# A six-stage transformer block on one core: the head of the first stage, the stores and the routing rearranged

## The reference, cut to what matters

```python
x = x + 0.5 * gated_moe(layernorm(x))     # 2 experts, top 1, silu(x Wg) * (x Wu), then Wd, FF 1024
x = x + attention(layernorm(x))           # 16 heads of 16, causal, softmax
x = x + 0.5 * gated_moe(layernorm(x))     # the same weights
x = x + 0.5 * moe(layernorm(x))           # 8 experts, top 2, logits = gelu(x rw1) @ rw2, gelu FF 1024
x = x + mixer(layernorm(x))               # a state-space mixer
x = x + 0.5 * moe(layernorm(x))           # the same weights as in stage 4
```

## Time and profile before

| | us |
|---|---|
| runs, median of 3 | 994.5 (992.1 to 997.3) |
| the profiled execution | 990.16 |
| its span | 988.3 |
| stage 1, gated MoE with weight preparation | to about 151 |
| stage 2, attention | to about 333 |
| stage 3, gated MoE | to about 452 |
| stage 4, MoE of 8 experts | to about 631 |
| stage 5, mixer | to about 804 |
| stage 6, MoE of 8 experts | to the end |

### The profile page before, as it was taken

One profiled execution on the slowest core, in us unless ns is written; L12 is line 12 of the kernel. 1 busy time (PEld: TensorE's weight loads), 2 busy tenths in 40 slices (PEclk: granted clock), 3 DMA queues, 4 the chain that ended last, 5 costly groups with the idle time before them and its releaser, 6 DMA issues.

```text
span 988.3 us, 21269 instructions
## 1 busy us (share of the span) xinstructions
PE 845.4 (86%) x7784; PEld 551.6 (56%) x7785; DVE 615.4 (62%) x1132; ACT 428.9 (43%) x990; POOL 337.2 (34%) x400
## 2 busy tenths in 40 slices
PE   3089988978888789998989999897889879999995
PEld 2046553423333336664689999544344444999993
DVE  5635646678993436654646565676798746555655
ACT  6434435136767515444244444367211152544440
POOL 2212114050000211112344553224888632555530
PEclk9999989989999879997799999999999997999997
DMA  8326622531104214422487664300000003666644
GB/s 292 130 86 213 220 73 75 174 109 48 27 20 172 78 32 144 131 94 92 163 335 242 239 226 155 100 1 1 0 1 0 1 30 115 252 242 238 226 156 142
DMA packets 46296, 125.38 MB, mean 127 GB/s; under 512 B 10202, under 2 KB 23467, under 8 KB 40207
## 3 DMA queue, kind: packets, MB, share of 16 engines
q0 software_dynamic: 13392, 67.96, 19.6%
q1 hardware_dynamic: 26698, 49.36, 15.2%
q10 hardware_dynamic: 6132, 7.05, 2.2%
HBM read 97.28 MB, written 26.71 MB: 125 GB/s over the span
## 4 chain that ended last, share of the span: by engine, by line
PE 57%; DVE 13%; DMA 9%; ACT 8%; POOL 6%; issue 6%; SPq 1%; ACTq 0%; DVEq 0%; POOLq 0%
PE psum L567 16%; PE psum L540 12%; PE psum L526 7%; PE psum L1347 3%; DMA stage<-in_w 3%; DVE mem L1472 2%; PE psum L114 2%; POOL mem L2137 2%; POOL mem L2133 2%; PE psum L513 1%; DMA mem<-xn_dram,mem 1%; PE psum L1900 1%; PE psum L1844 1%; DVE mem L312 1%; DMA max_dram<-mem 1%
## 5 line engine op out<-in xcount | busy, mean ns | idle before, releaser
L567 PE MATMUL psum<-mem 128*128 x1536 | 180.9, 275 | 3.2 <-DVE mem L808 1.9
L567 PEld LDWEIGHTS psum<-mem 128*128 128x128 f16 x1536 | 147.4, 98 | 24.4 <-issue 4.3
L540 PE MATMUL psum<-mem 128*128 128x128 f16 x2208 | 132.0, 220 | 0.0
L916 POOL DMA_INDIRECT y_dram<-mem x64 | 63.5, 993 | 194.5 <-DVE mem L824 194.5
L658 ACT ACTIVATE mem<-psum,mem 128x128 f32<-128x128 f32 x368 | 105.0, 369 | 54.3 <-PE psum L540 52.8
L540 PEld LDWEIGHTS psum<-mem 128*128 128x128 f16 x2208 | 128.1, 98 | 0.7
L911 POOL DMA_INDIRECT mem<-xn_dram,mem x64 | 66.7, 1042 | 120.5 <-PE psum L513 92.4
L1432 ACT ACTIVATE mem<-psum 128x512 f32<-128x512 f32 (+1 forms) x160 | 79.9, 552 | 54.3 <-PE psum L1327 35.5
L526 PE MATMUL psum<-mem 128*128 x432 | 100.3, 390 | 2.2 <-issue 2.2
L114 PE MATMUL psum<-ones 128*128 128x512 f16 x312 | 97.9, 440 | 0.6 <-issue 0.6
L1472 DVE TENSOR_REDUCE mem<-psum 128x2 f32<-128x1024 f32 (+2 forms) x96 | 87.6, 950 | 15.8 <-PE psum L1293 8.7
(11 more groups left out here) (246 smaller groups left out, 1382.1 us busy)
## 6 DMA issues: line engine op xcount, KB each, us to landing
stage<-in_w SPq DMA_DIRECT2D x32, 512.0 KB, 4.0
w_rows<-mem SPq DMA_DIRECT2D x8, 1024.0 KB, 7.6
xn_dram<-mem ACTq DMA_DIRECT2D x32, 128.0 KB, 1.7
mem<-y_dram SPq DMA_DIRECT2D x16, 256.0 KB, 5.2
mem<-in_w_gate SPq DMA_DIRECT2D x4, 512.0 KB, 6.7
mem<-in_w_up SPq DMA_DIRECT2D x4, 512.0 KB, 10.6
mem<-in_w_down SPq DMA_DIRECT2D x4, 512.0 KB, 14.0
mem<-y_dram SPq DMA_DIRECT2D x16, 128.0 KB, 3.4
```

Of the source, the lines that this page charges most:

```text
L540: ins = eng.matmul(c.bank(2 * p + j // half)[:, j % half * P:(j % half + 1) * P], mats[q][:, l, k, j * P:(j + 1) * P], x[:, p, k, :], star ...
L567: ins = eng.matmul(c.bank(6)[:, 0:D], a[:, 0 if gated else p, q * half + j, :], w[:, at], start=(i == 0), stop=(i == 3 * CF - 1))
L916: eng.indirect_dma_start(c.y_dram[:, :], bass.IndirectOffsetOnAxis(ap=yidx[:, b:b + 1], axis=0), yo[:, b % 2, :], None).then_inc(s_ys[b % ...
```

## The change

First stage. VectorE prepares gate and up, then does `block_x(0)` and `block_x(1)`, and only then the down matrix; TensorE's `block_ready` asks for gate and up alone, and the second product waits for down. The four attention matrices join `split1`, which now has 21 chunks; of each step's chunks the first two are handled where they were, a third behind `block_x` on ScalarE and behind `block_y` on VectorE. No store of w1 rows stands among the loads: the first is issued ahead of the attention stage, three behind its last maxima.

Routing. The router's matmuls go partly between the layer norm's transposes; ranks are computed with fewer and wider matmuls; the last expert's column is left out of the comparison and the clamp with it; the one-hot is made by two `tensor_tensor` on f16; activation tables are asked for early by an activation on one unused column.

Attention. The first key projection goes between the layer norm's transposes; GpSimd stores the first group of projected rows, SyncE only the second; stack 2 is asked for after the second half of pair 0's maxima has landed; `keep_awake` goes from 12 to 2 and from 2 to 1 a piece.

```diff
@@ layernorm_stage
     def act(eng):
+        if table is not None:
+            eng.activation(c.spent[:, 0:1], c.ln_consts[:, 0:1], table)
...
             ins.then_inc(s_tps.sem, 1)
+            worked = between(eng, i) if between is not None else 0
             if "idle_bank" in src:
-                keep_awake(c, eng, src["idle_bank"], 3)
+                keep_awake(c, eng, src["idle_bank"], 3 - min(worked, 2))
@@ moe_stage
+    def router_between(eng, i):
+        if i == 4:
+            for ready in W["router_ready"]:
+                eng.wait_ge(*ready)
+        if gated:
+            if i >= 4:
+                for n in ((0, 1, 2) if i == 4 else (i - 2,)):
+                    router_tile(eng, n)
+            return 0
+        if i < 5:
+            return 0
+        eng.wait_ge(*L["lo"](NT // 2))
+        ins = router_half(eng, 0, range(2 * (i - 5), 2 * (i - 4)))
+        if i == NT - 1:
+            ins.then_inc(s_hid.sem, 1)
+        return 2
...
-            for s in range(HALVES):
-                eng.wait_ge(*L["lo"]((s + 1) * NT // HALVES))
...
+            eng.wait_ge(*L["lo"](NT))
+            router_half(eng, 1, range(len(ROUTER))).then_inc(s_hid.sem, 1)
...
-        for t in range(NT):
-            out = c.bank(5)[:, NE + t * E:NE + (t + 1) * E]
-            todo = [(c.before16, k, t) for k in range(TOPK)] + [(c.ones16, k, u) for u in range(t) for k in range(TOPK)]
-            for i, (m, k, u) in enumerate(todo):
-                ins = eng.matmul(out, m[:, :], mk[:, k, u, :], start=(i == 0), stop=(i == len(todo) - 1))
+        ranks = c.bank(5)[:, NE:2 * NE].rearrange("p (t e) -> p t e", e=E)
+        for k in range(TOPK):
+            ins = eng.matmul(ranks, c.before16[:, :], mk[:, k, :, :], start=(k == 0), stop=False, skip_group_check=True)
+        for u in range(NT - 1):
+            for k in range(TOPK):
+                ins = eng.matmul(ranks[:, u + 1:NT, :], c.ones16[:, :], mk[:, k, u, :].unsqueeze(1).to_broadcast([P, NT - 1 - u, E]),
+                                 start=False, stop=(u == NT - 2 and k == TOPK - 1), skip_group_check=True)
...
+        if weights_act is None:
+            eng.activation(c.spent[:, 1:2], c.ln_consts[:, 0:1], ACT.Silu if gated else ACT.Gelu)
...
-        eng.tensor_scalar(ebi[:, :], ebf[:, :], float(E - 1), None, ALU.min).then_inc(s_eb.sem, 1)
         if not gated:
-            link(eng.tensor_scalar(spare[:, :], ebf[:, :], float(E - 1), float(P), ALU.min, ALU.mult))
-            eng.tensor_scalar(widx[:, :], spare[:, :], c.row_spare[:, :], float(1 + TOP2 * T), ALU.add, ALU.subtract).then_inc(s_wi.sem, 1)
-            eng.wait_ge(*s_wi(1))
+            eng.tensor_scalar(widx[:, :], ebf[:, :], float(P), c.row[:, :], ALU.mult, ALU.add).then_inc(s_wi.sem, 1)
+        eng.tensor_copy(ebi[:, :], ebf[:, :]).then_inc(s_eb.sem, 1)
...
-        for i in range(KT):
-            eng.tensor_scalar(oh[:, i, :], c.iota_p[:, :], pcol[:, i // NT, i % NT:i % NT + 1], None, ALU.is_equal)\
-                .then_inc(s_oh.sem, 1)
+        columns = pcol[:, :, :].rearrange("p k t -> p (k t)")
+        for i in range(2):
+            part = slice(i * KT // 2, (i + 1) * KT // 2)
+            eng.tensor_tensor(oh[:, part, :], c.iota16[:, 0:P].unsqueeze(1).to_broadcast([P, KT // 2, P]),
+                              columns[:, part].unsqueeze(2).to_broadcast([P, KT // 2, P]), ALU.is_equal).then_inc(s_oh.sem, 1)
...
         block_x(0, 0)
         block_x(1, 1)
+        if weights_late is not None:
+            weights_late(eng)
@@ attention_stage
+    def first_keys(eng, i):
+        if i < 5:
+            return 0
...
+    L = layernorm_stage(c, src, XN, between=first_keys)
...
         first_stack(eng, "wq", 0)
-        for e in range(KD):
-            for j, m in enumerate(("wk", "wq")):
...
+        store_rows(eng, 1)
         guard_rows(eng, 1)
...
-        store_w1(eng, 2)
-        store_w1(eng, 3)
+        for i in range(1, 4):
+            store_w1(eng, i)
...
-        keep_awake(c, eng, 4, 12)
+        keep_awake(c, eng, 4, 2)
...
             maxima(p, n)
-            keep_awake(c, eng, 4, 2)
+            keep_awake(c, eng, 4, 1)
...
         eng.wait_ge(*s_pd[0](16 * 6))
-        for p in range(1, STACKS - 1):
-            stacks(eng, p)
+        stacks(eng, 1)
+        eng.wait_ge(*s_ms[1](16))
+        stacks(eng, 2)
...
     def pool(eng):
         L["pool"](eng)
+        store_rows(eng, 0)
@@ program
-                  second=(down_h, down_l), block_ready=[first["done"](first["count"])], first_time=True, idle=8, bias_part=None)
+                  second=(down_h, down_l), block_ready=[first["done"](3)], second_ready=[first["done"](first["count"])], first_time=True, idle=8, bias_part=None)
...
-        split1 = split_weights(c, [(A["rw1"], flat(rr_h), flat(rr_l)), (A["w1"], w1_h, w1_l)], stage,
-                               after=split0["done"](split0["count"]))
+        split1 = split_weights(c, [*mat_jobs, (A["rw1"], flat(rr_h), flat(rr_l)), (A["w1"], w1_h, w1_l)], stage,
+                               after=first["done"](first["count"]))
...
-                               (lambda eng: (first["act"](eng), split0["act"](eng))) if n == 0 else None,
-                               (lambda eng: (first["dve"](eng), split0["dve"](eng))) if n == 0 else None,
-                               (lambda eng: (split0["sync"](eng), load_w1(eng))) if n == 0 else None)
+                               first["act"] if n == 0 else None,
+                               (lambda eng: (first["low"](eng, 0), first["low"](eng, 1))) if n == 0 else None,
+                               (lambda eng: first["low"](eng, 2)) if n == 0 else None,
+                               load_w1 if n == 0 else None)
```

More of the change, by code:

```diff
@@ L114, in keep_awake, with layernorm_stage @@
         eng.matmul(c.bank(bank), c.ones16[:, :], wide, start=True, stop=True)
-def layernorm_stage(c, src, XN, stored=None, lead=True):
+def layernorm_stage(c, src, XN, stored=None, lead=True, between=None, table=None):
     s_st = c.sem("ln_st", NT)
@@ L330, in stored, with router_tile, router_half @@
         eng.dma_start(c.xn_dram[1 + t * P:1 + (t + 1) * P, :], XN[:, t, :]).then_inc(s_xs.sem, 16)
-    L = layernorm_stage(c, src, XN, stored, W["bias_part"] is None)
     order = src["order"]
+    def router_tile(eng, n):
+        t = order[n]
+        eng.wait_ge(*L["lo"](n + 1))
+        tok = slice(t * P, (t + 1) * P)
+        i = 0
+        for k in range(KD):
+            for a, b in ((c.XTh, W["gh"]), (c.XTh, W["gl"]), (c.XTl, W["gh"])):
+                ins = eng.matmul(c.bank(5)[:, t * E:(t + 1) * E], a[:, k, tok], b[:, k, :],
+                                 start=(i == 0), stop=(i == 3 * KD - 1))
+                i += 1
+        return ins
+    ROUTER = [(k, a, b) for k in range(KD) for a, b in (("r1h", c.XTh), ("r1l", c.XTh), ("r1h", c.XTl))]
+    def router_half(eng, s, steps):
+        tok = slice(s * BANK, (s + 1) * BANK)
+        for i in steps:
+            k, a, b = ROUTER[i]
+            ins = eng.matmul(c.bank(s), W[a][:, k, :], b[:, k, tok], start=(i == 0), stop=(i == len(ROUTER) - 1))
+        return ins
+    def router_between(eng, i):
[14 more added lines that the diff above has]
+        return 2
+    L = layernorm_stage(c, src, XN, stored, W["bias_part"] is None, router_between, None if gated else ACT.Gelu)
     NE = NT * E
@@ L2289, in within, with part, act, dve @@
         def within(split):
-            def act(eng, b):
-                for i in chunks_of(split["count"], b):
+            def part(b, late):
+                chunks = chunks_of(split["count"], b)
+                return chunks[2:] if late else chunks[:2]
+            def act(eng, b, late):
+                for i in part(b, late):
                     split["high"](eng, i)
-            def dve(eng, b):
-                for i in chunks_of(split["count"], b):
+            def dve(eng, b, late):
+                for i in part(b, late):
                     split["low"](eng, i)
@@ L2303, in load_w1 @@
             for i in range(split1["count"]):
-                for part in range(2):
-                    if i == 2 + 4 * (part + 1):
-                        store_w1(eng, part)
                 split1["load"](eng, i)
```

110 lines of the change are left out of this document (59 added, 51 removed).

## The result

The changed kernel took 964.7 us (median of 4 runs, 962.0 to 966.3); the kernel before took 993.5 beside it (4 runs, 992.1 to 997.3). The ratio is 0.9715, with a 95% interval of 0.9668 to 0.9761: faster. The forecast was 966.9, with a range of 960 to 975. Of the two profiled executions the one of 990.2 is faster than all four runs of its kernel, and the one of 966.3 is the slowest of its own, so that their spans differ by only 23.9, against 27.6 in the sum of the prediction. The intervals of the ratios leave out one execution each of b_control (988.9), b_bridge_sync (991.3) and d_both (1247.8), in which the chip was in a slower state; the first two are the profiled ones, and their traces are read only up to stage 4.

The account below looks back on a forecast made before the run. TensorE was busy 845.4 of 988.3 us; only waits that leave it idle could be won. Stage 1 18.3, attention 3.4, stage 3 0.5, stage 4 3.1, stage 6 2.3: 27.6 off the median 994.5 gives 966.9, range 960 to 975.

Parts of the forecast that it names:

- The first block: Stage 1: first matmul of the blocks at 38.6 instead of 52.09 us, 13.5 won.
- The last block: End of stage 1: 10.3 us from the step before's second product become 6.1, 4.2 won.
- The steps: Stage 1: 0.65 lost for each step behind a late chunk, less than was lost before, 0.6 won.
- Attention: Attention's head: maxima start earlier and the second half's store lands sooner, 3.4 us won by the first exponentials.
- rival (a): Attention gives nothing, as small maxima transfers queue behind stack 2: 970.3 us, chance 0.15.
- The routing: Stages 4 and 6, each: router matmuls 1.0, VectorE operations 0.45, one-hot 0.85 won; stage 3: 0.5 won.
- rival (b): The one-hot is faster, with f16 operands at two columns a cycle: 964.4 us, chance 0.15.
- Stages 4 and 6 behind `idx`: Early activation tables: 0.8 won in stage 4 at an awaited gather behind a slab, 0 in stage 6.
- (c): Rows stored late at attention's end, so stage 3's VectorE waits: 971.9 us, chance 0.05.
- (d): Slower: chunk loads bound stage 1, 986 us at 8.75 a load, 1009 at 12; chance 0.02.
- (e): Stage 1's new order does nothing, as held gathers hold the first block: 13.5 missing, 980.4 us, chance 0.03.

Follow-up runs that it names:

- b_control: The changed kernel itself, run once more unedited for comparison on another chip: ratio 0.9739 against the kernel before.
- b_bridge_sync: Changed kernel with SyncE asking for stack 2 behind pair 0's maxima, 2 `keep_awake` between maxima and 12 behind the last: ratio 0.9759 against the kernel before.
- d_both: Changed kernel with ScalarE asking for stack 2 behind the first unit's exponentials, and gathers ahead of weight slabs: 962.2 us, ratio 0.9689 against the kernel before.
- c_stack2_act: Changed kernel with stack 2 asked for by ScalarE behind the first unit's exponentials: ratio 0.9701 against the kernel before.
- c_chunks_early: Changed kernel with a step's third chunk handled with the other two, ahead of the next block's gate: 977.0 us, ratio 0.9861 against the kernel before.
- a_low_first: Changed kernel with the third weight matrix's low half back ahead of the first block's halves on VectorE: ratio 0.9776 against the kernel before.

## Why the prediction was right, and where it was not

**The first block, 13.5**: right to 0.1 (38.70). Its way was right too: two low halves, a gather held until the second ends, 1.5 for the rows, a turn.

**The last block, 4.2**: the second product of the step before ended at 121.10 and the last one at 127.21, 6.1 as worked out. **The steps, 0.6**: what is left is 19.1 - 13.4 - 4.2 = 1.5. Late chunks cost 0.8 instead of 2.6; mis-sized was the 0.65 for each step behind one, which was 0.26 in the step shown above. Some of it went again in the first step, 10.6 us instead of 8.95: its product took 6.74 us instead of 5.34, at a granted clock of 0.68 in the window from 50 to 53, and for this I had no term. Against this the first product of all took 6.81 instead of the 7.75 that I had left it.

**Attention, 3.4**: this is the step that failed. Its parts up to the landing nearly held: 2.8 at the first reduction (3.3 foreseen), 3.9 at the second half's landing (4.5), both from the last tile's low half. The prediction then charged 1.1 for ScalarE's issue. What stood there was rival (a), the way back behind stack 2 (3.79 instead of 1.92 without it), at 2.1; and after it a longer ramp, 1.9, which no step had; that is the lower clock (14.0 instead of 12.2 without the held operation). I had costed the removed `keep_awake` by their time alone and never asked what clock the work behind them would get. Rival (a) had 0.15 and names half of the truth. Mending its half alone (c_stack2_act) brought 1.1 at the first pair's end and nothing at the eighth's.

**The routing**: operations and one-hot 1.3 in each of stages 4 and 6, as foreseen (0.45 + 0.85), though not by these parts: in stage 6 of the kernel before, 8.28 us pass from the router's result to the one-hot and in the changed kernel 7.95, so 0.3; the one-hot gave 1.1 (4.10 to 2.96); and 0.2 went behind it, where `idx` comes 0.69 after the one-hot's end instead of 0.51. The router's half gave 0.8 instead of 1.0 in both stages: from the last tile's low half to the first operation on the result 3.31 us instead of 4.15. The mechanism of the one-hot was right: one side waits for the other. Its size was 2.96 instead of 2.45 + 0.81 = 3.25, since the product needed 0.66 of its own and not 0.81. The Trainium skill, "GPSIMD Engine Reference", section "Key points", says that GpSimd shares SBUF interfaces with VectorE's two-input instructions; the trace agrees, 2.35 against 2.96. By the rule of the Trainium skill, "VectorE: DVE Perf Modes", in its text on choosing the mode, I had expected no double speed for an operand that is one value repeated; the trace agrees, 1.18 us for 1024 columns where the f32 instruction of the earlier trace rows took 1.22, and rival (b) is out. In stage 3 what the routing won was lost again by the first `turn_h`: the first product took 7.94 us instead of 7.05, at a mean granted clock of 0.67 instead of 0.76.

**Stages 4 and 6 behind `idx`**: 2.0 won in stage 4 (0.8 foreseen), where a wait of 3.03 became two of 0.56 and 1.55; then 1.6 less at stage 6's router (22.9 after 24.5): from the last second product of stage 4 on it takes 199.4 us instead of 197.8, although the router's half wins 0.8 there, so 2.4 are lost in stage 5 and around it, which I did not trace; and in stage 6 a new wait of 1.56 for a gather behind a slab, because the rows are asked for sooner. I had written 0 for it.

**The other rivals**: (c) no; the eight stores of 1 MB had a median of 8.8 us from issue to landing, and transfers fell from 395 GB/s (301 to 303) to 47 (303 to 305), some 10 us ahead of attention's last additions (313.9). (d) no; loads took 3.9, far from 8.4. But c_chunks_early shows the danger to be near: a chunk that stands ahead of the gate costs 2.2, late it costs 0.2. (e) no, though a_low_first shows that 2.2 of the third low half's 4.4 were hidden behind gathers.

So 966.9 against 964.7 is closer than its terms deserve: the profiled spans say 3.7 too much, mostly attention, and the median of the kernel before lies 3.3 above its profiled run while that of the change lies 1.6 below its own.

## What to carry to other kernels

With two buffers, a third chunk in a step belongs behind all that the step's last consumer waits for; a chunk's price is its load, not its arithmetic (2.2 against 0.2 us a step). Before removing idle matmuls ahead of a thin stretch, add to their own time what the stretch takes at the lower clock: here 2.3 won and 1.9 lost in the ramp. And a small transfer on a critical path is to be asked for before a large one on the same or a neighbouring queue: 8 KB took 11.55 us behind 393 KB, and 1.95 with nothing ahead. And a short two-input operation of VectorE on the path should not fall into two-input work of GpSimd: here this cost up to 1.5 us.

## What was not expected

An indirect gather's issue on GpSimd is held by a long two-input instruction on VectorE to its end (4.02 and 3.80 us beside one of 4.4, 0.94 alone). It holds the other way round too, and for the shortest instructions: an operation of VectorE that takes 0.17 us took up to 1.66, to the end of GpSimd's two-input instruction. VectorE's reductions from PSUM were not held (1.23 us in the change, 195.30, while GpSimd was at the same work). The granted clock differs between executions of the same instructions by enough to matter: a mean of 0.56 or of 0.76 in the same ramp, 2 us of time, and 1.00 or 0.81 in the second pair, 2.7 us. And on two of four chips stage 4's blocks, the same code, took 142 to 150 us instead of 138 to 139.
